# Local attention by 64-row halves of TensorE: 64x64 segment products in two banks for 128x128 products

## What is computed

```python
B, S, D, H, DK, DV, SEG = 2, 512, 256, 16, 128, 128, 64
def step(carry, seg):                       # one segment of 64 tokens, in sequence
    mem, z = carry
    qq, kk, vv = seg
    scores = jnp.einsum('bhsk,bhtk->bhst', qq, kk) / scale
    scores = jnp.where(causal_mask, scores, -jnp.inf)
    att_dot = jax.nn.softmax(scores, axis=-1) @ vv          # local attention
    att_mem = sigma_q @ mem / (sigma_q @ z)
    delta = vv - sigma_k @ mem / (sigma_k @ z)
    mem_new = mem + jnp.einsum('bhsk,bhsv->bhkv', sigma_k, delta)
    z_new = z + sigma_k.sum(axis=-2, keepdims=True).transpose(0, 1, 3, 2)
    att = beta * att_mem + (1.0 - beta) * att_dot
    out = att.reshape(Bsz, SEG, H * DV) @ Wo
```

## Time and profile before

| | us |
|---|---|
| median of 3 runs | 751.22 |
| lowest and highest | 750.45, 751.37 |
| the profiled execution | 748.37 |
| its span, from first to last instruction | 746.6 |
| PE busy (share of the span) | 651.1 (87%) |
| PE's weight loads busy | 541.0 (72%) |
| DVE busy | 413.5 (55%) |
| ACT busy | 339.7 (45%) |
| POOL busy | 313.6 (42%) |

### The profile page before, as it was taken

The page is one execution under the profiler, slowest core; times in us unless marked ns, Lnnn a source line. Parts: engine busy times, 40 slices in busy tenths (PEclk is TensorE's granted clock), DMA queues, the critical chain, the costliest instruction groups (busy, mean ns, idle before and its releaser), DMA issues. The chain is left out here.

```text
span 746.6 us, 12362 instructions
## 1 busy us (share of the span) xinstructions
PE 651.1 (87%) x4144; PEld 541.0 (72%) x4144; DVE 413.5 (55%) x1119; ACT 339.7 (45%) x834; POOL 313.6 (42%) x383
## 2 busy tenths in 40 slices
PE   4889989989989989989989986999999619984897
PEld 3668878979979879879879885876666307874564
DVE  6778495394494493692692737662222268455243
ACT  3566757557566556666665651223333302100220
POOL 4665644344353444435421213336665317210563
PEclk9999999999999999999999998999999859995798
DMA  8010110100100100100100313962332242019440
GB/s 271 14 58 29 34 53 1 64 29 3 62 29 25 40 28 28 35 28 28 36 2 1 98 50 107 406 227 85 93 92 78 76 142 86 1 34 357 130 121 19
DMA packets 31313, 57.89 MB, mean 78 GB/s; under 512 B 4670, under 2 KB 17952, under 8 KB 31264
## 3 DMA queue, kind: packets, MB, share of 16 engines
q1 hardware_dynamic: 24256, 42.03, 16.4%
q0 software_dynamic: 4896, 13.12, 6.1%
q10 hardware_dynamic: 2112, 2.10, 0.8%
HBM read 48.06 MB, written 10.09 MB: 78 GB/s over the span
## 5 line engine op out<-in xcount | busy, mean ns | idle before, releaser
L894 DVE RECIPROCAL denominators<-readings 128x2 f32<-128x2 f32 x128 | 21.2, 166 | 148.8 <-PE readings L567 148.1
L567 PEld LDWEIGHTS readings<-memory_copy,sigma 128*128 128x128 f32 x512 | 75.2, 191 | 14.2 <-ACT memory_copy L766 5.4
L427 POOL TENSOR_TENSOR w_high<-xn,ones 128x256 fp32r<-128x256 f32 x84 | 52.5, 655 | 77.0 <-PE ahead L215 35.7
L567 PE MATMUL readings<-memory_copy,sigma 128*128 128x129 f32 x512 | 79.1, 277 | 4.1 <-ACT memory_copy L766 3.8
L775 ACT ACTIVATE memory_reading<-readings,denominators 64x128 f32<-64x128 f32 x256 | 78.5, 356 | 5.2 <-DVE denominators L894 3.1
L766 ACT ACTIVATE memory_copy<-memory 128x258 f32<-128x258 f32 x128 | 50.2, 393 | 62.3 <-PE memory L577 48.2
L900 DVE SCALAR_TENSOR_TENSOR minus_delta<-readings,denominators,v 64x128 f32<-64x128 f32 x240 | 73.8, 347 | 4.2
L577 PE MATMUL memory<-minus_delta,sigma_k_tokens 128*128 128x129 f32 x480 | 73.3, 275 | 0.0
L751 ACT ACTIVATE x<-ahead 128x512 f32<-128x512 f32 x60 | 35.8, 597 | 76.8 <-DVE sigma L883 30.1
L1343 PE MATMUL up_e<-weights_e,xT_e 128*128 x184 | 69.9, 505 | 0.8 <-ACT xT_e L1467 0.8
L1198 POOL DMA_INDIRECT xs_e<-rows_e,gather_at_e x46 | 44.8, 974 | 59.9 <-DVE scatter_at_e L1599 36.1
(11 more groups left out here) (267 smaller groups left out, 1430.0 us busy)
## 6 DMA issues: line engine op xcount, KB each, us to landing
weights_e<-experts SPq DMA_DIRECT2D x24, 608.0 KB, 11.9
xn<-L_attn_Wq SPq DMA_DIRECT2D x8, 512.0 KB, 3.8
xn<-L_attn_Wk SPq DMA_DIRECT2D x7, 512.0 KB, 3.9
xn<-L_attn_Wv SPq DMA_DIRECT2D x7, 512.0 KB, 3.7
wo<-L_attn_Wo SPq DMA_DIRECT2D x1, 2048.0 KB, 12.9
rows_e<-xn ACTq DMA_DIRECT2D x4, 512.0 KB, 8.0
x<-L_attn_x SPq DMA_DIRECT2D x4, 256.0 KB, 3.7
x<-L_attn_x SPq DMA_DIRECT2D x2, 512.0 KB, 3.6
```

The source lines that it names most:

```text
L427: last = pool.tensor_tensor(w_high[i][:, :, of], w_stage[:, :, of], one, ALU.mult)
L567: last = pe.matmul(KQ[g][:, hh * MC:(hh + 1) * MC], sqk[:, GROUP * g + hh, pair, 2 * par:2 * par + 2, :], mz[g][:, hh, :], start=True, sto ...
```

## The change

A product takes the 64 keys of one segment (64 rows of `v`, all 128 value columns) and multiplies them with the 64 queries of the same segment (64 rows and 64 columns of `pTs`). Even segments lie on rows 0 to 63 and odd ones on rows 64 to 127; the products alternate between these halves. A half's results go to a bank of their own, `L[par]`, in which both heads of the pair stand beside each other. So a pair of heads has 16 products where it had 8. PE waits once for both heads' copied probabilities, and signals `bt_ready` once a pair. ACT waits once, then makes four scaled copies of 256 columns, two from each bank, each of which writes the 64-column stretches of `att` that belong to its segments; `bt_copied` rises after each bank, so it still counts four a stage. SP's wait has the new count.

```diff
@@ block.sync
-                sp.wait_ge(bt_ready, 4 * STAGES)
+                sp.wait_ge(bt_ready, 2 * STAGES)
@@ block.tensor
-                def local(n, half, pp, hh):
-
-                    h = GROUP * pp + hh
-                    pe.wait_ge(pTs_ready, 4 * n + h + 1)
-                    for t in range(TPH):
-                        last = pe.matmul(L[hh][:, t * P:(t + 1) * P], v[:, half * TPH + t, h * DK:(h + 1) * DK],
-                                         pTs[hh][:, t * P:(t + 1) * P], start=True, stop=True)
+                def local(n, half, pp):
+                    pe.wait_ge(pTs_ready, 4 * n + GROUP * pp + GROUP)
+                    for hh in range(GROUP):
+                        h = GROUP * pp + hh
+                        for t in range(TPH):
+                            for par in range(2):
+                                rows, at = slice(par * SEG, (par + 1) * SEG), (hh * TPH + t) * SEG
+                                last = pe.matmul(L[par][:, at:at + SEG], v[rows, half * TPH + t, h * DK:(h + 1) * DK],
+                                                 pTs[hh][rows, t * P + par * SEG:t * P + (par + 1) * SEG],
+                                                 start=True, stop=True)
                     last.then_inc(bt_ready, 1)
...
                     if m in (10, 14):
-                        for hh in range(2):
-                            local(n, half, (m - 10) // 4, hh)
+                        local(n, half, (m - 10) // 4)
@@ block.scalar
                 def scale_local(n, half, pp):
 
-                    for hh in range(2):
-                        h = GROUP * pp + hh
-                        act.wait_ge(bt_ready, 4 * n + h + 1)
-                        act.activation(att[:, half, h, :], L[hh][:, :], ACT.Copy, scale=one_less_q[:, h:h + 1])\
-                           .then_inc(bt_copied, 1)
+                    act.wait_ge(bt_ready, 2 * n + pp + 1)
+                    for par in range(2):
+                        for hh in range(GROUP):
+                            h = GROUP * pp + hh
+                            last = act.activation(
+                                att[:, half, h, :].rearrange("p (t a c) -> p t a c", a=2, c=SEG)[:, :, par, :],
+                                L[par][:, hh * TPH * SEG:(hh + 1) * TPH * SEG].rearrange("p (t c) -> p t c", c=SEG),
+                                ACT.Copy, scale=one_less_q[:, h:h + 1])
+                        last.then_inc(bt_copied, 1)
```

## The result

| | before | changed |
|---|---|---|
| median of 6 runs, us | 751.57 | 759.80 |
| lowest to highest, us | 750.45 to 754.23 | 757.69 to 761.88 |
| the profiled execution (span), us | 748.37 (746.6) | 761.88 (760.1) |
| matmul passes and loads, each | 4144 | 4400 |

The ratio is 1.0089, with a 95% interval of 1.007 to 1.0109: the change costs 8.2 us. I forecast slower, 759.1 us, within 752 to 772.

The account below looks back on a forecast made before the run. PE's queue was taken to bound attention. Regrouping the array (5.4 us), the merged wait (2.2) and ACT's copies (0.3) sum to 7.9 us, the body gaining nothing: median 759.1 us, range 752 to 772 us.

Parts of the forecast that it names:

- PE's queue: In attention, PE sets the pace, busy 50.8 of 54 us a stage; its waits on DVE don't soak up losses.
- merged wait: Before a block's first load, PE waits for both heads' copied probabilities: +0.24 us in 8 slots, 2.2 us in sum.
- Body: A local block's 32 passes run as 16 pairs of row halves at 0.112 us: 1.79 us, no gain.
- exit: Return from the divided array to whole-array work after each local block: +0.14 us.
- rival 1: In local blocks, the row halves' loads run one by one: 28.6 us more, 787.7 us; chance 0.15.
- Entry: Regrouping from whole-array work to the divided array before each local block: +0.20 us.
- Stage 0's slot 14: Only here in the slots 14 does waiting for the second copy delay the first load: 0.29 us beyond the regrouping's 0.20.
- ACT: Four scaled copies take 1.54 us, +0.29 us a block, covered except in the last stage: +0.3 us on the path.
- The sum: Whole kernel: 5.4 + 2.2 + 0.3 = 7.9 us more; profiled execution 756.3 us, median 759.1 us.
- rival 2: In local blocks, pairs of loads go at the scores' pace, 0.066 us: faster than before, 747.4 us; chance 0.04.
- rival 3: Around local blocks, regrouping costs nothing or PE's waits on DVE absorb it: 2.5 us left, 753.7 us; chance 0.09.
- Rival 4: In local blocks, row halves pair only in part, as both passes of a product queue together: 760 to 773 us; chance 0.07.

Follow-up runs that it names:

- The second visit: Changed kernel with each block cut in two, head 1's products moved to the slot's end; 759.96 us against 748.49 for the kernel before, ratio 1.0146.

## Why the prediction held

- **PE's queue is the bound of attention, and nothing absorbs what it loses.** Right. PE's waits on DVE kept their size to 0.4 us, and the merged wait alone moved attention by 4.1 us for 3.9 put in.
- **Body, 1.79 us, the halves in pairs, the 128-column load as floor.** Right. The block of 1.93 us is 16 rounds and the exit. Whole rows with the same 64 columns gave 3.57 us, and one half alone 3.71 us, which is rival 1's case (3.58 and the exit). The value was read from column halves (scores), and row halves behave alike.
- **Entry 0.20, exit 0.14.** Right: 0.20 us in slot 14, and 1.93 against 1.78 us for the body with its exit, 0.15. The second visit showed that it is a price for each visit, 0.31 us there.
- **Merged wait, 2.2 us.** Right: undoing it in the slots 10 gave 1.9 us. Stage 0's slot 14, with 0.29 us of the sum, wasn't tried in the changed kernel; its first load was 0.37 us behind the start of the last L577 pass before and is 0.86 behind it now, the 0.20 and 0.29 that I counted.
- **ACT.** Right: 1.54 us for four copies, covered in every stage but the last, where the wait grew by 0.3 us. The stride cost nothing that the rows show.
- **The sum.** 7.9 us, of which attention's stretch and its end show 8.1. The median moved by 8.2. That the medians agree to 0.3 us is in part luck: the kernel before had medians of 748.49 to 751.57 us in different sets of runs. The 8.1 us of attention don't hang on it. My figure for the profiled execution, 756.3 us, was 5.6 us short of the 761.88 of the one that was profiled; what is missing lies outside attention, and the runs of one kernel spread over 4 us. That spread of the later stages was in the range, not in the sum.
- **The rivals.** Rivals 1 and 2 are excluded by the block's 1.93 us and rival 3 by its entry. Rival 4, pairs that form only in part, doesn't occur in the order of the change, but is real in a coarser one: runs of four and eight products took 2.53 and 3.32 us.

What I didn't see in the prediction is that rival 2's rate was to be had: not with halves, but with quarters, whose 64-column loads the scores' rows had already priced.

## What to carry to other kernels

For a small f32 product count loads and moving columns apart: the time of a pass is the larger, and halving the smaller one wins nothing. Dividing the array pays where the larger one is halved too, and each visit among whole-array work cost 0.31 to 0.35 us here, so put many passes into one visit and alternate the parts, with no run of one part over about four passes. A wait that is merged on the engine that sets the pace costs what it waits; look whether the engine that it waits for has the work in the right order.

## What the runs showed beyond that

- Four quarters of the array took loads 0.016 us apart (64 in 1.02 us), each load being of 64 columns; two halves of rows 0.058 us (32 of 128 columns in 1.86 us).
- The granted clock fell to 1.2 GHz in stretches where PE was busy all the time, within or behind blocks of 3.3 to 3.7 us that used one half of the rows at a time; with runs of 8 products it cost about 20 us of attention. Blocks of the same length on all rows, and blocks with runs half as long, kept 2.4 GHz.
- PE took up work of another part from about four passes behind in its queue, and from sixteen behind it did not.
